# AdaLN cross-attention on one core: a new prologue, with six value and key tiles made inside steps 0 to 2

## What is computed

```python
ss = silu(c) @ W_ss + b_ss                       # for the query side and for the key/value side
xq  = (1 + scale_q)  * layernorm(x)   + bias_q
xkv = (1 + scale_kv) * layernorm(ctx) + bias_kv
q = xq @ Wq + bq;  k, v = split(xkv @ Wkv + bkv)
attn = softmax(q @ k.T / sqrt(32))               # 64 keys for each row and head
out = x + (attn @ v) @ Wp + bp
```

## Time and profile before

| | |
|---|---|
| median of 3 runs | 1185.86 us (1185.43 to 1186.97) |
| the profiled execution | 1185.47 us |
| its span | 1183.7 us |
| PE busy | 1140.7 us, 96% of the span |
| DVE, ACT, POOL busy | 86%, 72%, 71% |
| chain that ended last | PE 86%, the rest on all others and on issue |
| mean granted clock | 0.986 |

### The profile page before, as it was taken

One profiled execution on the slowest core, in us unless ns is written; L12 is line 12 of the kernel. 1 busy time (PEld: TensorE's weight loads), 2 busy tenths in 40 slices (PEclk: granted clock), 3 DMA queues, 4 the chain that ended last, 5 costly groups with the idle time before them and its releaser, 6 DMA issues.

```text
span 1183.7 us, 32530 instructions
## 1 busy us (share of the span) xinstructions
PE 1140.7 (96%) x11072; PEld 696.6 (59%) x11072; DVE 1019.2 (86%) x1799; ACT 858.0 (72%) x1624; POOL 840.1 (71%) x941
## 2 busy tenths in 40 slices
PE   7798699999999999999999999999999999999997
PEld 2665366566665666656666566566665666656653
DVE  4745698989989889898898988989889899898895
ACT  2477577778777777777777777777787777787653
POOL 1543486877778786868787786868687777869555
PEclk9798799999999999999999999999999999999999
DMA  8111113223223232232322323223232232232222
GB/s 331 70 36 36 63 64 100 99 90 106 89 97 106 80 106 90 96 106 80 106 92 94 106 80 106 97 89 106 81 105 97 90 106 86 100 107 65 72 73 80
DMA packets 59871, 112.00 MB, mean 95 GB/s; under 512 B 6412, under 2 KB 6440, under 8 KB 59832
## 3 DMA queue, kind: packets, MB, share of 16 engines
q1 hardware_dynamic: 59832, 111.48, 27.6%
HBM read 77.90 MB, written 33.55 MB: 94 GB/s over the span
## 4 chain that ended last, share of the span: by engine, by line
PE 86%; issue 2%; POOL 2%; ACT 1%; DVE 0%; POOLq 0%; ACTq 0%; DVEq 0%
PE ps_q L1135 27%; PE ps_o L1203 26%; PE ps_t L1169 11%; PE ps_v L1188 8%; PE ps_s L1154 8%; PE ps_v L1118 4%; POOL xr L418 1%; PE ps_o L1135 0%; POOL xr L394 0%; PE ps_v L1082 0%; POOL half_den L425 0%; POOL xh L385 0%; PE ps_t L1118 0%; DVE xT_lo L847 0%; ACT xT_hi L510 0%
## 5 line engine op out<-in xcount | busy, mean ns | idle before, releaser
L394 POOL TENSOR_TENSOR xr<-xr,bp_row 128x512 f32<-128x512 f32 x128 | 163.1, 1274 | 155.9 <-ACT junk L583 155.9
L885 DVE TENSOR_REDUCE mx<-ps_s 128x8 f32<-128x512 f32 x256 | 164.8, 685 | 90.8 <-PE ps_s L1154 90.4
L425 POOL TENSOR_TENSOR half_den<-pr 128x512 f32<-128x512 f32 x128 | 162.8, 1272 | 64.6 <-ACT pr L612 35.0
L558 ACT CAST pt_hi<-ps_t 128x512 f16<-128x512 f32 x256 | 137.6, 589 | 92.5 <-PE ps_t L1169 92.5
L568 ACT ACTIVATE q_hi<-ps_q,cur_bq 128x512 f16<-128x512 f32 x126 | 86.5, 687 | 133.0 <-PE ps_q L1135 110.1
L418 POOL TENSOR_TENSOR xr<-y,xr 128x512 f32<-128x512 f32 x128 | 162.4, 1269 | 6.5 <-ACT y L535 6.5
L905 DVE TENSOR_TENSOR pt_lo<-ps_t,pt_hi 128x512 f16<-128x512 f32 x256 | 163.3, 679 | 0.0
L877 DVE SCALAR_TENSOR_TENSOR pr<-pr,ps_v 128x512 f32<-128x512 f32 x256 | 162.8, 675 | 0.0
L897 DVE TENSOR_TENSOR pr<-ps_s,mx 128x512 f32<-128x512 f32 x256 | 161.9, 673 | 0.0
L612 ACT ACTIVATE pr<-pr,exp_scale 128x1024 f32<-128x1024 f32 x128 | 146.4, 1144 | 16.4 <-DVE pr L897 16.4
L1169 PE MATMUL ps_t<-ident,pr 128*128 128x128 f32 x1024 | 140.9, 281 | 4.7 <-DVE pr L877 4.7
(11 more groups left out here) (162 smaller groups left out, 2292.7 us busy)
## 6 DMA issues: line engine op xcount, KB each, us to landing
x_in<-in_x_dram SPq DMA_DIRECT2D x128, 256.0 KB, 2.7
xr<-in_x_dram SPq DMA_DIRECT2D x128, 256.0 KB, 2.9
out_dram<-xr SPq DMA_DIRECT2D x128, 256.0 KB, 2.0
raw<-in_L_xcond_Wss_kv_dram SPq DMA_DIRECT2D x4, 512.0 KB, 5.0
cx<-in_ctx_dram SPq DMA_DIRECT2D x1, 2048.0 KB, 12.1
raw<-in_L_xcond_Wss_q_dram SPq DMA_DIRECT2D x4, 512.0 KB, 12.8
...
```

The source lines that it names most:

```text
L394: pool.tensor_tensor(xr[:, s, :], xr[:, s, :], bp_row[:, :], ALU.add).then_inc(xr_ready, 1)
L425: pool.tensor_tensor(half_den[:, :, :], pr[:, off % 2, :, 0:LKV // 2], pr[:, off % 2, :, LKV // 2:LKV], ALU.add).then_inc(half_done, 1)
L885: dve.tensor_reduce(mx[:, HALF * h:HALF * (h + 1)], ps_s[:, h, :].rearrange("p (h l) -> p h l", l=LKV), AX_X, ALU.max)\
```

## The change

- The context's first half is loaded first and in pieces; the five small loads go to ACT's queue. The modulations' weights are loaded by columns.
- `modulate` uses the weights as the stationary operand and silu of c as 16 moving columns: 8 blocks of 4 products, whose result lies already turned. ACT's copies and PE's turns of it are gone. The query side's modulation stands between key tiles 0 and 1.
- The limit is made twice: for keys and values (`limits(0)`) and for query and output (`limits(1)`), eight columns each.
- The context's second half is normalised by POOL; rows 0 to 3 of x get their moments and normalisation from DVE, not from ACT and POOL.
- wv's and wk's halves are made in pieces, and the products wait for the pieces. Four value tiles and then the key tiles follow in blocks; tiles use banks of all of PSUM. Values are made in two halves of 256 columns, even and odd heads, on ACT and on DVE, and 4 DMAs of SP a tile place them (`place_values`) in place of the eight copies.
- Value tiles 5, 6, 7 and key tiles 5, 6, 7 are made in steps 0 to 2 (`late_tiles`, `late_keys`), with their operations on DVE, ACT and POOL.

```diff
+        def chunk_bank(n):
+            return (ps_t[:, 0, :], ps_t[:, 1, :], ps_q[:, :])[n % TURNED]
+        def value_bank(t):
+            return (ps_s[:, 0, :], ps_s[:, 1, :], ps_v[:, 0, :], ps_v[:, 1, :], ps_v[:, 0, :], ps_t[:, 0, :],
+                    ps_t[:, 0, :], ps_o[:, :])[t]
+        def key_bank(n):
+            return (ps_s[:, 0, :], ps_s[:, 1, :], ps_v[:, 0, :], ps_v[:, 1, :], ps_v[:, 1, :], ps_t[:, 1, :],
+                    ps_t[:, 1, :], ps_o[:, :])[n]
...
+        def late_tiles(b, i):
+            return ((5,), (6, 7), ())[i] if isinstance(b, int) and b == 0 and i < 3 else ()
+        def late_keys(b, i):
+            return ((5,), (6,), (7,))[i] if isinstance(b, int) and b == 0 and i < 3 else ()
...
-            sp.dma_start(c_row, cond).then_inc(ld_small, 16)
-            for at, v, n in ((BSSQ, bss_q, 2 * KC), (BSSKV, bss_kv, 2 * KC), (BQ, bq, KC), (BK, bkv, 2 * KC)):
-                sp.dma_start(brow[at:at + n, :], v.rearrange("(r c) -> r c", c=P)).then_inc(ld_small, 16)
-            for k in range(KC):
-                sp.dma_start(wss[0][:, k, :], Wss_kv[P * k:P * (k + 1), :]).then_inc(ld_ss[k], 16)
-            sp.dma_start(cx, ctx_in.rearrange("b l d -> (b l) d").rearrange("(t p) d -> p t d", p=P)).then_inc(ld_ctx, 16)
-            for k in range(KC):
-                sp.dma_start(wss[1][:, k, :], Wss_q[P * k:P * (k + 1), :]).then_inc(ld_ssq[k], 16)
+            ctx_rows = ctx_in.rearrange("b l d -> (b l) d").rearrange("(t p) d -> p t d", p=P)
+            def load_context(j):
+                sp.dma_start(cx[:, 2 * j:2 * j + 2, :], ctx_rows[:, 2 * j:2 * j + 2, :]).then_inc(ld_ctx[j], 16)
+            def load_modulation(side, w, landed):
+                rows = w.rearrange("(k p) n -> p k n", p=P)
+                for c in range(KC):
+                    cols = slice(2 * P * c, 2 * P * (c + 1))
+                    sp.dma_start(wss[side][:, :, cols], rows[:, :, cols]).then_inc(landed[c], 16)
+            load_context(0)
+            load_context(1)
+            load_modulation(0, Wss_kv, ld_ss)
             sp.dma_start(wv_raw, Wkv[:, H:2 * H].rearrange("(k p) n -> p k n", p=P)).then_inc(ld_wv, 16)
+            load_context(2)
+            load_context(3)
+            sp.dma_start(wk_raw, Wkv[:, 0:H].rearrange("(k p) n -> p k n", p=P)).then_inc(ld_wk, 16)
             sp.dma_start(wq[:, :, :], Wq.rearrange("(k p) n -> p k n", p=P)).then_inc(ld_wq, 16)
-            sp.dma_start(wk_raw, Wkv[:, 0:H].rearrange("(k p) n -> p k n", p=P)).then_inc(ld_wk, 16)
-            sp.dma_start(bp_row[:, :], bp.rearrange("(a n) -> a n", a=1).partition_broadcast(P)).then_inc(ld_bp, 16)
+            load_modulation(1, Wss_q, ld_ssq)
+            sp.dma_start(wp_raw, Wp.rearrange("(k p) n -> p k n", p=P)).then_inc(ld_wp, 16)
...
+            def place_values(t):
+                sp.wait_ge(v_lo_done, 2 * t + 2)
+                for hb in range(2):
+                    for par in range(2):
+                        sp.dma_start(v_all[LKV * par:LKV * (par + 1), :, 2 * t + hb, :, :],
+                                     v16[LKV * hb:LKV * (hb + 1), :, t % 2, par, :]
+                                     .rearrange("p s (g d) -> p s g d", d=DH)).then_inc(v_placed[t % 2], 16)
...
+                context_hi(0)
+                value_weights_hi(0)
+                context_hi(1)
+                value_weights_hi(1)
+                context_hi(2)
+                context_hi(3)
+                sum_of_squares(wv_raw, ld_wv, 0, 1, squares[0])
+                sum_of_squares(wk_raw, ld_wk, 0, 0, squares[0])
+                key_weights_hi(0)
+                key_weights_hi(1)
+                act.wait_ge(wv_done, KC)
+                sum_of_squares(wq[:, :, :], ld_wq, 1, 0, squares[1])
+                for n in range(KC):
+                    value_hi(n)
+                    context_hi(KC + n)
+                key_hi(0)
+                sum_of_squares(wp_raw, ld_wp, 1, 1, squares[1])
+                for n in range(1, KC):
+                    key_hi(n)
+                    if n == 2:
+                        scaled_wq_hi(0, 0)
+                scaled_wq_hi(0, 1)
+                act.wait_ge(wv_done, KC)
+                turned_x(0, 0)
+                turned_x(0, 1)
+                scaled_wq_hi(0, 2)
+                turned_x(0, 2)
+                turned_x(0, 3)
+                scaled_wq_hi(0, 3)
+                act.wait_ge(masks_ready, 2)
+                key_blocks(0)
+                act.wait_ge(bq_ready, 2)
+                query_bias(0)
+                row_moments(4)
+                value_hi(4)
+                row_moments(5)
+                query(0, 0, first_banks[0])
+                turned_x(0, 4)
+                key_hi(4)
+                row_moments(6)
+                query(0, 1, first_banks[1])
+                turned_x(0, 5)
+                row_moments(7)
+                query(0, 2, first_banks[0])
+                turned_x(0, 6)
+                row_moments(8)
+                query(0, 3, first_banks[1])
+                turned_x(0, 7)
+                row_moments(9)
...
+                for n in range(KC):
+                    context_chunk(n)
+                    if n > 0:
+                        value_weights_lo(n - 1)
+                value_weights_lo(3)
+                context_stats(1)
+                limits(0)
+                limits_top(0)
+                key_weights_lo(0)
+                key_weights_lo(1)
+                limits_copy(0)
+                key_weights_lo(2)
+                key_value_scales()
+                key_weights_lo(3)
+                for n in range(KC):
+                    value_lo(n)
+                    context_chunk(KC + n)
+                modulation(1)
+                limits(1)
+                keys(0)
+                first_stats()
+                keys(1)
+                limits_top(1)
+                first_rows(0)
+                first_rows(1)
+                keys(2)
+                limits_copy(1)
+                first_rows(2)
+                first_rows(3)
+                query_output_scales()
+                query_bias()
+                keys(3)
+                first_wq_lo(0)
+                turned_x(0, 0)
+                first_wq_lo(1)
+                turned_x(0, 1)
+                turned_x(0, 2)
+                first_wq_lo(2)
+                turned_x(0, 3)
+                output_bias()
+                first_wq_lo(3)
...
             def modulate(side, landed):
-                for k in range(KC):
-                    pe.wait_ge(landed[k], 16)
-                    for a in range(2):
-                        last = pe.matmul((ps_s, ps_v)[side][0:B, a, :], silu_t[:, k, :],
-                                         wss[side][:, k, H * a:H * (a + 1)], start=(k == 0), stop=(k == KC - 1))
+                dst = (ps_v[:, 1, :], ps_o[:, :])[side]
+                for m in range(2 * KC):
+                    pe.wait_ge(landed[m // 2], 16)
+                    for k in range(KC):
+                        last = pe.matmul(dst[:, B * m:B * (m + 1)], wss[side][:, k, P * m:P * (m + 1)],
+                                         silu_t[:, k, :], start=(k == 0), stop=(k == KC - 1))
                 last.then_inc(mod_mm, 1)
...
-            modulate(0, ld_ss)
-            turn_modulation(0)
-            modulate(1, ld_ssq)
-            pe.wait_ge(mod_ready, 2)
-            turn_context(0)
-            turn_modulation(1)
-            pe.wait_ge(mod_ready, 4)
-            for m in range(KC):
-                turn_context(m + 1)
-                if m == 0:
-                    pe.wait_ge(ld_wq, 16)
-                shift_product(m)
-            turn_context(5)
...
+                for t in late_tiles(b, i)[:1]:
+                    value_rows(t)
+                for n in late_keys(b, i):
+                    key_rows(n)
+                for t in late_tiles(b, i)[1:]:
+                    value_rows(t)
             def prime():
+                for n in range(TURNED):
+                    turn_context(n)
+                modulate(0, ld_ss)
+                turn_context(3)
                 value_rows(0)
+                value_rows(1)
+                limits_turn(0)
+                value_rows(2)
+                limits_spread(0)
+                value_rows(3)
+                for n in range(KC, 2 * KC - 1):
+                    turn_context(n)
                 key_rows(0)
+                pe.wait_ge(lim_copied, 1)
+                modulate(1, ld_ssq)
+                turn_context(2 * KC - 1)
+                key_rows(1)
+                pe.wait_ge(mod_ready, 4)
+                limits_turn(1)
+                key_rows(2)
+                limits_spread(1)
+                pe.wait_ge(ld_wq, 16)
+                pe.wait_ge(c_mul, CT)
+                for m in range(KC):
+                    shift_product(m)
+                key_rows(3)
+                for f in range(FIRST):
+                    turn_x(0, f)
+                value_rows(4)
```

(7 more changed lines are left out.)

658 lines of the change are left out of this document (338 added, 320 removed).

## The result

The changed kernel takes **1199.9 us** (median of 4 runs, 1199.6 to 1203.7) against 1186.4 for the kernel before (4 runs beside them, 1185.4 to 1187.6): a ratio of 1.012, 95% interval 1.0098 to 1.0143. It is 13.5 us slower, where 1185.0 was forecast and the range ended at 1194. The profiled execution has a span of 1197.9 us against 1183.7, so 14.2 are to be found in it.

What follows compares the result with a forecast made beforehand. PE bounds the kernel at 8.2 us a step, unchanged; only prologue and start-up move. First score 108.5 plus steps 46.25 put the fifth score at 154.7, 0.8 earlier than 155.5: 1185.0 us, range 1178 to 1194.

Steps and rivals of the forecast that it cites:

- The five small loads on ACT's queue: Prologue start: loads ahead of ACT's table load cost 0 to 1 us, hidden by the context's landing.
- With 4.3 from 13.5 the stage runs 2.4 us at half and 6.5 at full: First modulation on PE: clock rises 4.3 us after PE restarts at 13.5; modulation runs from 15.4 to 24.3.
- The rival named for this: Both modulations and key product 1: thin products leave PE at half clock; 1194.5 us, chance 0.28.
- The values' limit: Prologue: keys' and values' limit, after value products 1 and 2, POOL's power and seven DVE operations, gives its scale at 47.4.
- The rounds: Prologue: four rounds of value high part, low part, chunk and cast, one behind the other on ACT and DVE, 3.7 us.
- The last chunk: Prologue: last context chunk, after the four rounds on ACT and DVE, ready at 61.4 us.
- fits inside this: Prologue: PE's second modulation, 7.8 us, fits inside the time until the last chunk is ready.
- The two gaps: Prologue: PE idles 2.9 us behind key product 1 and nearly 4 before x's turn 2; slow clock adds 1.7 and 2.3.
- Steps 0 and 1: Start-up: two moved products in step 0, 9.4 us, and three in step 1, 12.2 us, covered on DVE and ACT.
- Step 2: Start-up: PE waits 5.6 us for the division behind wp's low part, then starts at half clock; 15.7 us.
- Step 3: Start-up: 8.2 us and 0.7 for DVE.
- the six products cost 9.8 of their 16.8 here: Steps 0 to 3: with the six moved products they take 46.25 us against 36.5 before.

Runs made afterwards that it cites:

- five moves: Changed kernel with small loads on SP, first modulation before context turns, POOL's four rows on DVE, Wp's square behind Wq's, wp's low part behind first division: 1188.7 us.
- the shift products' run: Changed kernel with five moves, earlier value high parts, last-chunk turn and row-12 load; shift products behind key product 3, x's turns 0-1 before query weights: 1183.1 us.

## Why the prediction was wrong

The forecast walked to a first score at 108.5 and a fifth at 154.7; they came at 119.5 and 169.7. The 15.0 us, by its own steps:

- **"The five small loads on ACT's queue ... cost 0 to 1 us, hidden"** failed: +3.1 at the start of the modulation (18.5, not 15.4). DVE takes silu ahead of the statistics, and silu waits for those loads. Undoing it gave 3.5 back.
- **"With 4.3 from 13.5 the stage runs 2.4 us at half and 6.5 at full"** failed: +4.7. It is the largest single step, but it doesn't decide the sign alone: by this sum the fifth score would still come 9.5 us later than before without it. I read the clock of 1.00 in the earlier trace rows as thin products holding it, and counted turns and thin products towards its rise. The runs show that they do neither: 40 us of them left it at half, and after dense products it fell within the modulation. The rival named for this (1194.5) was the right mechanism and somewhat too dear: it priced 5.7, 2.3 and 1.5 for the first modulation, the second and key product 1, and the trace has 4.7, 0.7 and 1.3 over the forecast.
- The values' limit came 0.7 us later than the steps ahead of it explain, so that chain of waits was right. The rounds were right too: 3.63 us against 3.7, with halves of 0.84 and 0.88 against the 0.85 that I chose.
- **The last chunk** was 3.4 us further behind. Two of PE's turns waited 2.2 us for context rows that POOL makes at 2.1 us each, and 1.1 of it reached DVE; I had not priced POOL's rows. And the last turn stands behind the second modulation on PE, which cost DVE 2.0; "fits inside this" was wrong. Both waits in DVE's timeline:

```profile
58.96 0.69 DVE L1084 TENSOR_TENSOR raw<-ps_t,sc_kv 128x512 f32<-128x512 f32 x1 [1.12 <-PE ps_t L1192]
71.90 0.69 DVE L1084 TENSOR_TENSOR raw<-ps_t,sc_kv 128x512 f32<-128x512 f32 x1 [1.98 <-PE ps_t L1192]
```

- **The two gaps**: the second was right (forecast nearly 4, measured 3.7). The first was 1.3 instead of 2.9, since key product 1 was late itself. From there to the first score the forecast was 0.9 too long in all: 1.3 for key product 1, then 1.7 less, 0.4 more and 0.9 less.
- **Steps 0 and 1**: 9.48 and 12.20 against 9.4 and 12.2. **Step 2**: the wait of 5.6 was 5.4, but the step took 18.7 instead of 15.7: turns and query product took 6.6 us instead of 5.3, most of it cold, and the 1.6 us wait for x's low part stands in the trace of before as well (1.7 us), where I did not look. **Step 3** was 0.9 longer, with 0.65 of it the same wait. So "the six products cost 9.8 of their 16.8 here" failed: in the changed kernel steps 0 to 3 are 13.7 longer than before, and against the run with all tiles in the prologue 15.9. The line of before:

```profile
146.49 0.30 PE L1188 MATMUL ps_v<-pt_hi,vb 128*64 128x128 f16 x4 [1.74 <-DVE xT_lo L847]
```


Sum: 3.1 + 4.7 + 0.7 + 3.4 + 1.3 - 1.7 + 0.4 - 0.9 = 11.0 ahead of the first score, and 4.0 in the steps. Of the chances, 0.38 for slower was fair, but the range stopped at 1194: it took the rival's price as an end, while the rival, the small loads and step 2 can all come together.

As for the change itself: its parts pull apart. Thin modulations alone cost the old kernel 10.9 us, with 5.2 of that a later start that the changed kernel doesn't have. In the changed kernel the first modulation's place behind the turns costs 6.8 and its form, with the place of its loads, another 2.5 (6.8 once the other chains are mended); the small loads cost 3.5, and the tiles in the steps bring at most 1.6. What the other parts (the split limit, placing by DMA, DVE's rows of x) bring was not tried one by one. The changed order can be 0.7% faster than before, once the first modulation and the chains are mended; that shows that the other parts together don't keep it slower, not that none of them costs anything. POOL's four rows and Wp's square were run only among five moves, so their own shares stay open, as does the share of each edit in the shift products' run.
